# Values' bias added by GpSimd in an SBUF buffer instead of by a matmul on PE; context tiles reordered on ACT and PE

## What is computed

```
x0    = layernorm(x)                       # "slots" start from it
x_in  = layernorm(ctx) * g + b
k     = x_in @ wk + bk
v     = x_in @ wv + bv                     # bv: the values' bias
slots = q_mu + exp(q_logsig) * x0
3 times:
    q      = layernorm(slots) @ wq + bq
    attn   = softmax(k @ q.T / scale) + 1e-8
    attn   = attn / attn.sum(over k's tokens)
    slots  = attn.T @ v @ wu + bu + slots
    slots  = layernorm(mlp(layernorm(slots)) + slots + cond)
x = x + slots
```

## Time and profile before

| | |
|---|---|
| median of 3 runs | 2355.93 us |
| the profiled execution, its own time | 2353.49 us |
| its span, first to last instruction | 2351.8 us |
| mean granted TensorE clock | 0.993 |
| PE busy | 2305.0 us (98%) |
| DVE busy | 1593.8 us (68%) |
| POOL busy | 998.0 us (42%) |
| ACT busy | 976.2 us (42%) |
| keys and values, half 1 to 7 on PE | from 83.6 to 255.8 us, 24.60 us a half |

### The profile page before, as it was taken

The page is one execution under the profiler, slowest core; times in us unless marked ns, Lnnn a source line. Parts: engine busy times, 40 slices in busy tenths (PEclk is TensorE's granted clock), DMA queues, the critical chain, the costliest instruction groups (busy, mean ns, idle before and its releaser), DMA issues. The chain is left out here.

```text
span 2351.8 us, 30910 instructions
## 1 busy us (share of the span) xinstructions
PE 2305.0 (98%) x11541; PEld 1895.1 (81%) x11541; DVE 1593.8 (68%) x2904; ACT 976.2 (42%) x1650; POOL 998.0 (42%) x1353
## 2 busy tenths in 40 slices
PE   8999999999999999999999999999999999899998
PEld 4888888888888888888888888888888887677886
DVE  7777666757477575778757667785775768875542
ACT  2565443333333333333333433434333345666432
POOL 1566235152453525435354452554535157743200
PEclk9999999999999999999999999999999999989999
DMA  5587000000052000013400001250000012204330
GB/s 202 193 309 263 1 1 1 1 1 5 32 205 78 1 23 5 14 50 126 152 6 15 13 10 55 108 170 5 10 19 1 19 50 86 73 28 135 103 112 19
DMA packets 87125, 158.58 MB, mean 67 GB/s; under 512 B 10801, under 2 KB 33337, under 8 KB 83134
## 3 DMA queue, kind: packets, MB, share of 16 engines
q1 hardware_dynamic: 82838, 150.26, 18.6%
q0 software_dynamic: 2688, 6.31, 0.9%
q10 hardware_dynamic: 1450, 0.04, 0.0%
HBM read 106.21 MB, written 50.37 MB: 67 GB/s over the span
## 5 line engine op out<-in xcount | busy, mean ns | idle before, releaser
L222 PE MATMUL ps<-zTh,kTl 128*128 128x512 f32 (+1 forms) x912 | 332.6, 365 | 8.4 <-DVE zTl L2052 5.7
L224 PE MATMUL ps<-zTh,kTh 128*128 128x512 f32 (+1 forms) x912 | 324.6, 356 | 0.0
L223 PE MATMUL ps<-zTl,kTh 128*128 128x512 f32 (+1 forms) x912 | 324.4, 356 | 0.0
L222 PE MATMUL ps<-vh,prob_lo 128*128 128x512 f32 x768 | 306.1, 399 | 0.0
L224 PE MATMUL ps<-vh,prob_hi 128*128 128x512 f32 x768 | 300.1, 391 | 0.0
L223 PE MATMUL ps<-vl,prob_hi 128*128 128x512 f32 x768 | 299.3, 390 | 0.0
L2530 POOL TENSOR_SCALAR rs_m<-mv_m 128x1 f32<-128x1 f32 x96 | 55.3, 576 | 544.1 <-DVE mv_m L2013 542.5
L2052 DVE TENSOR_TENSOR zTl<-ps,zTh 128x512 fp32r<-128x512 f32 x224 | 151.3, 683 | 198.4 <-ACT zTh L1779 198.4
L1914 ACT ACTIVATE prob<-ps,nb 128x1024 f32<-128x1024 f32 x96 | 107.3, 1117 | 256.6 <-DVE nb L2360 246.0
L222 PEld LDWEIGHTS ps<-zTh,kTl 128*128 128x128 f32 x912 | 172.1, 189 | 42.1 <-DVE zTl L2052 14.0
L1761 ACT ACTIVATE zbuf<-slots,rs_m 128x512 f32<-128x512 f32 x96 | 78.4, 817 | 303.4 <-POOL rs_m L2535 303.4
(11 more groups left out here) (332 smaller groups left out, 5701.1 us busy)
## 6 DMA issues: line engine op xcount, KB each, us to landing
ctx<-in_ctx_dram SPq DMA_DIRECT2D x8, 1024.0 KB, 7.8
slots<-in_x_dram SPq DMA_DIRECT2D x8, 1024.0 KB, 6.6
kT_d<-kTh SPq DMA_DIRECT2D x6, 1024.0 KB, 7.9
kT_d<-kTl SPq DMA_DIRECT2D x6, 1024.0 KB, 9.9
s_d<-slots SPq DMA_DIRECT2D x6, 1024.0 KB, 5.1
v_d<-vh SPq DMA_DIRECT2D x6, 1024.0 KB, 9.8
v_d<-vl SPq DMA_DIRECT2D x6, 1024.0 KB, 11.8
kTh<-kT_d SPq DMA_DIRECT2D x3, 2048.0 KB, 10.3
```

Of the source, the lines that this page charges most:

```text
L222: nc.tensor.matmul(out, ll, rh, start=start, stop=False)
L223: nc.tensor.matmul(out, lh, rl, start=False, stop=False)
L224: return nc.tensor.matmul(out, lh, rh, start=False, stop=stop)
```

## The change

1. PE: the 13th matmul of the value units goes, and with it `value_bias`, `vb_row`, `two` and their DVE work. A bank now counts as free when ACT has read it, for values too.
2. ACT: a value is copied from PSUM to one of three SBUF buffers (`kv_raw`); later, when GpSimd has added the bias there, `kv_hi` makes the high part from the buffer. The keys use two of the same three buffers.
3. POOL: `add_bias(h, u)`, one add of a 128x512 tile and a row, for u = 4 to 7 of each half.
4. DVE: `kv_lo` of a value reads buffer and high part, both in SBUF, and stands later; those of units 6 and 7 stand in the next half.
5. ACT takes the high parts of units 6 and 7 in the next half, behind the first two `c_norm`; `c_hi` of tiles 0 and 1 stands a unit later, and PE turns the tiles after units 1, 2, 3, 5 instead of 0, 1, 3, 5.

```diff
+    kv_buf = [gbuf[:, 0, :], gbuf[:, 1, :], tbuf[:, 1, :]]
+    KV_BUF = (0, 1, 0, 1, 2, 0, 1, 2)
+    KV_AGO = (3, 3, 2, 2, 5, 3, 3, 3)
...
                     if n >= 6:
-                        hb, ub = divmod(n - 6, 8)
-                        if ub < 4:
-                            pe.wait_ge(sem("kv_read"), 4 * hb + ub + 1)
-                        else:
-                            pe.wait_ge(sem("kv_lo"), n - 5)
+                        pe.wait_ge(sem("kv_read"), n - 5)
...
-                    if u >= 4:
-                        pe.wait_ge(sem("row_step"), 3 * (C + 1) + 5)
-                        last = nc.tensor.matmul(bank(n % 6), two[:, :], vb_row[:, :], start=False, stop=True)
...
-                    turned = ((0, 1, 3, 5) if h else (2, 3, 4, 5))
+                    turned = ((1, 2, 3, 5) if h else (2, 3, 4, 5))
...
+            def kv_raw(h, u):
+                n = 8 * h + u
+                act.wait_ge(sem("kv_done"), n + 1)
+                if n >= KV_AGO[u]:
+                    act.wait_ge(sem("kv_lo"), n - KV_AGO[u] + 1)
+                if u < 4:
+                    A.activation(kv_buf[KV_BUF[u]], bank(n % 6), ACT.Identity, bias=gr1[:, u:u + 1],
+                                 scale=cols["gq"][:, u:u + 1]).then_inc(sem("kv_read"), 1)
+                else:
+                    A.activation(kv_buf[KV_BUF[u]], bank(n % 6), ACT.Copy).then_inc(sem("kv_read"), 1)
...
+                    act.wait_ge(sem("v_added"), 4 * h + u - 3)
+                    A.activation(v[0][:, 4 * nh + u - 4, :], kv_buf[KV_BUF[u]], ACT.Copy).then_inc(sem("kv_hi"), 1)
...
             for h in range(1, HS - 1):
                 c_norm(h + 1, 0); c_norm(h + 1, 1)
+                kv_hi(h - 1, 6); kv_hi(h - 1, 7)
                 kv_hi(h, 0)
...
-                kv_hi(h, 4)
+                kv_raw(h, 4)
                 x_norm(h, 2)
-                kv_hi(h, 5)
+                kv_raw(h, 5); kv_hi(h, 4)
                 c_hi(h + 1, 3)
-                kv_hi(h, 6)
+                kv_raw(h, 6); kv_hi(h, 5)
                 x_norm(h, 3)
-                kv_hi(h, 7)
+                kv_raw(h, 7)
...
-                V.tensor_tensor(lo, gbuf[:, u % 2, :] if u < 4 else bank(n % 6), hi.bitcast(f32), ALU.subtract)\
-                    .then_inc(sem("kv_lo"), 1)
+                V.tensor_tensor(lo, kv_buf[KV_BUF[u]], hi.bitcast(f32), ALU.subtract).then_inc(sem("kv_lo"), 1)
...
                 x_stats(h, 0); x_stats(h, 1)
+                kv_lo(h - 1, 6); kv_lo(h - 1, 7)
...
+            def add_bias(h, u):
+                n = 8 * h + u
+                pool.wait_ge(sem("kv_read"), n + 1)
+                G.tensor_tensor(kv_buf[KV_BUF[u]], kv_buf[KV_BUF[u]], rows[:, 2, :], ALU.add).then_inc(sem("v_added"), 1)
...
-                first_slots(h, 0)
-                first_slots(h, 1); first_slots(h, 2)
+                first_slots(h, 0); first_slots(h, 1)
+                if h == HS - 1:
+                    first_slots(h, 2); first_slots(h, 3)
+                    add_bias(h, 4); add_bias(h, 5)
+                    rstd_z0(h)
+                    add_bias(h, 6); add_bias(h, 7)
+                    continue
+                add_bias(h, 4)
+                first_slots(h, 2)
+                add_bias(h, 5)
                 if h + 2 < HS:
                     rstd_c(h + 2)
+                add_bias(h, 6); add_bias(h, 7)
                 first_slots(h, 3)
```

More of the change, by code:

```diff
@@ L1593, in _ @@
                         else:
-                            mm3(pe, bank(n % 6), pair(zT, ALL, c, cut(4 * nh + u - 4)), pair(m2, ALL, c, ALL),
-                                c == 0, False)
-                    if u >= 4:
-                        pe.wait_ge(sem("row_step"), 3 * (C + 1) + 5)
-                        last = nc.tensor.matmul(bank(n % 6), two[:, :], vb_row[:, :], start=False, stop=True)
+                            last = mm3(pe, bank(n % 6), pair(zT, ALL, c, cut(4 * nh + u - 4)), pair(m2, ALL, c, ALL),
+                                       c == 0, c == C - 1)
                     last.then_inc(sem("kv_done"), 1)
@@ L1783, in c_hi @@
                 hi_transposed("c", 4 * h + i, i, 4 * (h % 2) + i)
+            def kv_raw(h, u):
[8 more added lines that the diff above has]
+                    A.activation(kv_buf[KV_BUF[u]], bank(n % 6), ACT.Copy).then_inc(sem("kv_read"), 1)
             def kv_hi(h, u):
                 n, nh = 8 * h + u, h % 2
[L1787 to L1793, removed]
-                A.activation(g, bank(n % 6), ACT.Identity, bias=gr1[:, u:u + 1],
-                             scale=cols["gq"][:, u:u + 1]).then_inc(sem("kv_read"), 1)
-                act.wait_ge(sem("kv_read"), 4 * h + u + 1)
-                if h >= 2 and u == 0:
-                    act.wait_ge(sem(f"kv_out{nh}"), h // 2 * 4 * 16)
-                A.activation(kT[0][:, u, cut(nh, 512)], g, ACT.Copy).then_inc(sem("kv_hi"), 1)
+                if u < 4:
+                    kv_raw(h, u)
+                    act.wait_ge(sem("kv_read"), n + 1)
+                    if h >= 2 and u == 0:
+                        act.wait_ge(sem(f"kv_out{nh}"), h // 2 * 4 * 16)
+                    A.activation(kT[0][:, u, cut(nh, 512)], kv_buf[KV_BUF[u]], ACT.Copy).then_inc(sem("kv_hi"), 1)
+                else:
+                    act.wait_ge(sem("v_added"), 4 * h + u - 3)
+                    A.activation(v[0][:, 4 * nh + u - 4, :], kv_buf[KV_BUF[u]], ACT.Copy).then_inc(sem("kv_hi"), 1)
             def x_norm(h, i):
@@ L1869, in _ @@
             z_hi(0, 0); z_normalize(0, 2)
-            kv_hi(h, 4)
+            kv_raw(h, 4)
             z_hi(0, 1); z_normalize(0, 3)
+            kv_raw(h, 5)
+            z_hi(0, 2)
+            kv_raw(h, 6); kv_hi(h, 4)
+            z_hi(0, 3)
             kv_hi(h, 5)
-            z_hi(0, 2)
-            kv_hi(h, 6)
-            z_hi(0, 3)
+            kv_raw(h, 7); kv_hi(h, 6)
             kv_hi(h, 7)
@@ L2145, in _ @@
             kv_lo(0, 2)
-            value_bias()
             fold(6)
@@ L2152, in _ @@
             c_stats(2, 0)
-            kv_lo(0, 4)
             dot_m(1, 2)
@@ L2209, in _ @@
             z_lo(0, 0)
-            kv_lo(h, 4)
+            z0_stats(h, 0)
             z_lo(0, 1)
-            z0_stats(h, 0); z0_stats(h, 1)
-            kv_lo(h, 5)
+            z0_stats(h, 1)
             z_lo(0, 2)
             z0_stats(h, 2); z0_stats(h, 3)
+            kv_lo(h, 4)
+            z_lo(0, 3)
+            kv_lo(h, 5)
             kv_lo(h, 6)
-            z_lo(0, 3)
             kv_lo(h, 7)
```

54 lines of the change are left out of this document (18 added, 36 removed).

## The result

| | before | after |
|---|---|---|
| median, runs on the same chip | 2354.96 us (2353.23 to 2356.59, 5 runs) | 2366.18 us (2364.44 to 2367.59, 5 runs) |
| ratio, with its 95% interval | | 1.0047 (1.0035 to 1.0058) |
| the profiled execution, its own time | 2353.49 us | 2367.01 us |
| its span | 2351.8 us | 2365.3 us |

The kernel became slower by 11.2 us; by the interval 8 to 14. The prediction's sign held, and its range, 2350 to 2368 us, holds the measured 2366. Its size did not: it said +5.3 us, so about half of the loss was foreseen, and 2366 lies halfway between the forecast, 2361, and its third rival, 2371.

A forecast was written before the change was run, and what follows sets the result against it. The prediction took PE, busy 98% of the span, as the bound, with a loop through GpSimd becoming longer than PE's half; -7.4 + 7.8 + 4.9 = +5.3 us on the median of 2355.93 gave 2361 us, range 2350 to 2368.

The forecast's parts named there:

- third rival: GpSimd and DVE block each other throughout: a turn of 27.7 us, +15 us in all, 2371 us; chance 0.10.
- Removed, -7.4 us: On PE, 32 bias matmuls of 0.23 us go, a half becomes 23.7 us; DVE's saved value_bias work in half 0 gains nothing.
- The adds themselves: On GpSimd, two bias adds ahead of the last pair on slots lengthen each turn by 2 x 1.30 = 2.6 us.
- The pair behind them: GpSimd's last pair on slots, behind two adds, slows beside DVE work with two SBUF inputs: +0.8 us a turn.
- DVE from the first context statistic to the last: DVE stretch of 9.25 us in each turn: +1.0 for two blocked operations, -0.6 for a low part leaving, +0.4 us.
- The sum over the halves: "+7.8": A turn of 25.6 us against PE's 23.7: PE loses 5.7 us in halves 3 to 5, 1.5 in 2, 0.6 in 6.
- The loop, named as the cause: GpSimd scale, adds, pair on slots, SP store, context load, DVE statistics, next scale: 21.8 us before, 25.6 us after.
- All three: ACT, DVE and GpSimd busy times in a half, said to stay under PE's 23.7 us, GpSimd at 21.8.
- The last half: "+4.9": Chains through GpSimd make PE wait 2.3 us for the first query tile, 0.7 behind it, 1.9 for tile 4.
- low-part waits of 0.7: In the last half, DVE's low parts of turned query tiles run late behind the first: 0.7 us in two waits.
- The signs that it named: What the changed profile should show: waits of PE and DVE, a later store, longer low parts, halves of 25.3 to 25.7 us.
- Rival 1: The loop is covered, the adds fit GpSimd's gaps, a turn is 23.7 us: -6 us, 2350 us; chance 0.16.

The follow-up runs named there:

- no_bias_mm: The kernel before with its 32 bias matmuls left out and nothing put in their place: 2346.1 us, ratio 0.9962 to the kernel before.
- ctx_first: The changed kernel with SP's load of a later context moved ahead of the store of slots: 2363.8 us, ratio 1.0037 to the kernel before.
- pair_first: The changed kernel with the last pair on slots ahead of the adds of units 6 and 7 again: 2372.1 us, ratio 1.0075 to the kernel before.
- low_psum: The changed kernel with DVE taking the values' low parts from PSUM, one input from SBUF: 2362.6 us, ratio 1.0040 to the kernel before.
- no_add67: The changed kernel without the bias adds of units 6 and 7 in halves 0 to 6: 2356.3 us, ratio 1.0007 to the kernel before.
- second profile: The changed kernel run and profiled once more, unchanged: 2365.8 us, ratio 1.0046 to the kernel before.
- col_spread: The changed kernel with the 32 one-column matmuls between halves 0 and 1 split into two pieces of 16: 2364.1 us, ratio 1.0039 to the kernel before.
- like pair of profiles: Repeats of the changed kernel (2365.8 us) and the kernel before (2354.7 us), both unchanged, both with a long half-clock stretch in half 1.
- no_end_adds: The changed kernel without the last six bias adds, units 6 and 7 of half 6 and all of half 7: 2359.1 us, ratio 1.0020.

## Why the prediction was right, and where its size was off

- **Removed, -7.4 us.** Right: no_bias_mm measured 7.5 us between medians and 23.69 us a half, forecast 23.7. `value_bias` was worth nothing, as said.
- **The adds themselves.** 2.49 us for two, forecast 2.6. The pair behind them took 3.43, forecast 3.39, and the load 7.3, forecast 7.4. All right.
- **DVE from the first context statistic to the last: the mis-sized step.** The prediction's "+0.4" (blocked instructions +1.0, one low part out -0.6) measured 10.30 - 9.25 = +1.05. Three instructions grew, not two: the low part of key 3 from 0.96 to 1.71 us, the last dot product from 1.03 to 1.60, the low part of value 4 from 0.66 to 0.95; +1.6, less the 0.6 that left. The two rows of the kernel before that are new here, DVE in half 3:

```profile
151.00 0.66 DVE L2075 TENSOR_TENSOR vl<-ps,vh 128x512 fp32r<-128x512 f32 x1
151.57 1.03 DVE L2067 CUSTOM_DVE_ANT_0 tbuf<-zc,rows 128x512 f32<-128x512 f32 x1
```

  In this stretch 1.3 of the 1.6 us are old instructions with two SBUF inputs, which the prediction had given 0.5. The turn became 26.05 instead of 25.6.
- **The sum over the halves: "+7.8".** Halves 2 to 6 are 128.58 us against 5 x 23.69 = 118.45: **+10.1**. Of the missing 2.3 us, 3 x 0.45 are the turn's length in halves 3 to 5. The rest are halves 2 and 6, which lost 1.9 and 1.1 us where 1.5 and 0.6 were forecast.
- **The loop, named as the cause: incomplete.** "All three stay under 23.7 us, so none is the bound by its sum; GpSimd, at 21.8, comes close." This is the step that failed. 21.8 was the old busy time, 16.6, and four adds at their undisturbed 1.30. Measured it is 23.67 us, as much as PE's own 23.69, with 1.6 us of waits left in a turn of 26.05, and two loops through GpSimd came out within 0.15 us of each other. In halves 3 to 5 ctx_first took the named loop away for 0.15 us, pair_first shortened it and lost 1.5 us a half more, low_psum took some of the blocking away and won about 1 a half, and no_add67 won 1.7 to 2.3. The sign came out right because the adds were put on the engine that both loops share.
- **The last half: "+4.9".** 28.47 - 23.69 + 1.46 = **+6.2**, in the second profile 27.87 - 23.69 + 1.49 = +5.7. The waits were 2.82 (forecast 2.3) and 1.46 (forecast 1.9); the low-part waits of 0.7 didn't come. New is a stretch at half clock right behind the 2.82 us wait (mean clock 0.66 from 251 to 256 us), some 1.7 us of PE's time, for which the prediction had no term. But that stretch is not what was lost. In col_spread PE ran the same place at full clock, half 7 took 27.62 us, and its wait for tile 4 was longer instead:

```profile
267.87 0.87 PE L1511 MATMUL ps<-ident,zbuf 128*128 128x128 f32 x4 [2.06 <-ACT zbuf L1825]
```

  That is 32.69 us into the half, against 32.81 in the changed kernel: tile 4 comes when GpSimd's chain is through, whatever PE's clock was. The prediction has that chain, and its undersized steps are the small instructions of the scales: the set for x took 2.7 us (forecast 2.0), the one before the last adds 2.4 (forecast 1.9). With them the last add ended 31.4 us in (forecast 30.0) and tile 4 came at 32.8 (forecast 31.4).
- **Sum of the measured terms:** -7.4 + 10.1 + 6.2 = +8.9 us, against +5.3. The like pair of profiles says 9.8, the medians 11.2 with an interval from 8 to 14. The remaining 1 to 2 us are not attributed; they are below what the runs can tell.
- **The signs that it named.** DVE's wait for the load: 2.05 us (said: about 1). SP's store 8.7 us into a half (said: 8 to 9). Low parts up to 1.77 us (said: 1.8). PE idle 1.5 to 2 us before halves 3 to 6: 1.79, 0.43, 1.84, 0.44; the two short ones end halves 3 and 5, in which PE's mean clock was 0.93. "Two waits of about 2 us" in half 7: 2.82 and 1.46. "Half 1 still 23.7": 26.58, wrong, by the clock.
- **The rivals.** Rival 1 (covered) lost to exactly the point that it gave, DVE waiting for the load. Rival 3 (blocking throughout) was wrong on the turn, 26.05 against 27.7, but right on the mechanism that the forecast under-priced, and its total, 2371 us, is as near to the measured 2366 as the forecast. That the range held owes something to that width; the sign came from the mechanism.

## What to carry to other kernels

Before work is moved to GpSimd, add its busy time as it will be when DVE runs instructions with two SBUF inputs beside it, for both engines and for old instructions as well as new, and compare that with the pace-setting engine; here an engine that waited only 1.6 us of a turn of 26 was already the bound, though another wait closed the loop in the trace. When one loop closes exactly in the measured time, look for a second within a few tenths before repairing it: here the obvious repair gave 0.15 us, and the opposite order cost 1.5. And look twice at a profile before a slow stretch of TensorE's clock is put down to a change.

A version that beats both was not found. With the bias left out altogether, as in no_bias_mm, the kernel is 0.4% faster. In the kernel as it stands that is the most that moving this add could win, and no order tried here on GpSimd wins any of it.

## What the runs showed of the hardware that was not expected

- A half with slack swallows a slow stretch of TensorE. In half 3 PE ran 3.4 us at 0.51 of full speed (1.2 GHz), from 1.6 us after its wait of 1.79 us, and its next wait was 0.43 us in place of 1.8; half 4, at clock 1.00, ended with a wait of 1.84. Both took 26.05 us. Such a stretch does not follow every wait of that length: in no_end_adds half 3 began behind a wait of 1.82 us and ran at clock 1.00. In the kernel before, where PE sets the pace in every half, the stretch in half 1 was paid: 27.14 against 24.74 us, with halves 2 to 7 at 24.60 in both. In the changed kernel half 2 gave 0.4 us of it back (25.63 against 26.06 in no_end_adds), and in the last half the wait for tile 4 took nearly all of it.
- The price of a GpSimd instruction is more than its undisturbed row. Over the kernel 32 adds of 1.30 us brought 50.1 us of GpSimd time, not 41.6, and DVE, with five instructions less, was busy 14 us longer. The longest ones hardly grew (pairs on `slots` 1.74 before and 1.81 after, keys' low parts 1.78 in both); more of them were long. `scale_w1` went from 1.57 to 2.00 us each time.
- Two profiles of one unchanged kernel differed by 2.4 us in one half, by the granted clock alone (24.74 and 27.14 us).
